# Six tiles in work in place of five, every engine's order and the PSUM banks written out per tile, early weights on ScalarE's DMA queue

## Time and profile before

| | |
|---|---|
| runs | 1672.52, 1680.17, 1679.59 us (median 1679.59) |
| profiled execution, first to last instruction (span) | 1672.2 us; the page gives no time beside it |
| TensorE busy | 1389.7 us, 83% |
| VectorE busy | 1370.5 us, 82% |
| ScalarE busy | 970.5 us, 58% |
| GpSimd busy | 721.2 us, 43% |
| mean granted TensorE clock | 0.956 |

### The profile page before, as it was taken

How to read it: one execution, slowest core, us unless ns; L and a number is a source line. 1 busy time by engine, 2 the same in 40 slices (tenths; PEclk the granted TensorE clock), 3 DMA queues, 4 the chain that set the end, 5 groups by cost and what they waited for, 6 DMA issues and landing times.

```text
span 1672.2 us, 42249 instructions
## 1 busy us (share of the span) xinstructions
PE 1389.7 (83%) x16237; PEld 973.1 (58%) x16270; DVE 1370.5 (82%) x4054; ACT 970.5 (58%) x1992; POOL 721.2 (43%) x1143
## 2 busy tenths in 40 slices
PE   2466789988888889999888889999888888997765
PEld 1344666666666666666565666666665666665432
DVE  4356798888988898888998898888988899887652
ACT  1134566666666666666566666666666666665432
POOL 4244454444544544444544544444544545442200
PEclk9888999999999999999999999999999999999875
DMA  6001111111111111111111110111111111111100
GB/s 211 10 8 28 39 25 34 43 43 43 30 43 42 42 28 29 43 43 43 30 43 43 43 32 25 43 43 43 33 39 43 42 37 23 29 33 31 28 24 4
DMA packets 130948, 64.36 MB, mean 38 GB/s; under 512 B 97591, under 2 KB 123575, under 8 KB 130494
## 3 DMA queue, kind: packets, MB, share of 16 engines
q1 hardware_dynamic: 130750, 61.66, 14.0%
HBM read 50.05 MB, written 2.14 MB: 31 GB/s over the span
## 4 chain that ended last, share of the span: by engine, by line
PE 46%; DVE 23%; POOL 11%; ACT 7%; issue 6%; SPq 4%; DMA 2%; POOLq 1%; DVEq 0%
PE ps_all L1332 7%; PE ps_all L1624 5%; PE ps_all L1458 5%; POOL rden L507 5%; POOL wide_a L507 4%; DVE mx L1013 4%; PE ps_all L1373 4%; PE ps_all L1444 4%; PE ps_all L1399 3%; DVE wide_b L1016 3%; PE ps_all L1325 3%; PE ps_all L1412 3%; DVE wide_b L1076 3%; POOL rstd L507 2%; DVE den L1061 2%
## 5 line engine op out<-in xcount | busy, mean ns | idle before, releaser
L507 POOL TENSOR_TENSOR rstd<-rstd,minus_half 128x1 f32<-128x1 f32 x320 | 175.6, 552 | 817.1 <-DVE rstd L991 814.1
L1013 DVE TENSOR_REDUCE mx<-ps_all 128x8 f32<-128x512 f32 (+1 forms) x192 | 163.8, 866 | 55.1 <-PE ps_all L1361 36.2
L507 POOL TENSOR_TENSOR rden<-rden,minus_half 128x16 f32<-128x16 f32 x64 | 187.7, 2933 | 9.4
L743 ACT COPY wide_a<-ps_all 128x512 f32<-128x512 f32 (+1 forms) x192 | 139.2, 725 | 88.4 <-PE ps_all L1412 72.7
L1332 PE MATMUL ps_all<-ident,wide_b 128*128 128x128 f32 x1024 | 156.4, 290 | 25.7 <-ACT wide_b L756 24.1
L507 POOL TENSOR_TENSOR wide_a<-wide_a,wide_b 128x256 f32<-128x256 f32 x256 | 177.7, 726 | 0.0
L1332 PEld LDWEIGHTS ps_all<-ident,wide_b 128*128 128x128 f32 x1024 | 121.4, 148 | 67.4 <-issue 34.2
L743 ACT COPY wide_c<-ps_all 128x512 f32<-128x512 f32 (+1 forms) x96 | 69.9, 728 | 118.3 <-PE ps_all L1332 118.3
L756 ACT ACTIVATE wide_b<-wide_b 128x512 f32<-128x512 f32 (+1 forms) x160 | 114.9, 718 | 23.8 <-DVE wide_b L1016 22.6
L1016 DVE TENSOR_TENSOR wide_b<-ps_all,mx 128x512 f32<-128x512 f32 (+1 forms) x160 | 126.0, 787 | 2.4
L1399 PE MATMUL ps_all<-w_qkv,ht_shift 128*128 128x512 f32 x256 | 124.1, 608 | 1.5 <-ACT ht_shift L766 1.5
(11 more groups left out here) (266 smaller groups left out, 3646.2 us busy)
## 6 DMA issues: line engine op xcount, KB each, us to landing
wide_a<-in_k SPq DMA_DIRECT2D x64, 256.0 KB, 3.1
wide_c<-wide_c SPq DMA_DIRECT2D x128, 64.0 KB, 2.2
v_pad<-in_v SPq DMA_DIRECT2D x32, 256.0 KB, 3.8
v_pair<-in_v SPq DMA_DIRECT2D x32, 136.0 KB, 2.7
ctx_t<-in_ctx_t SPq DMA_DIRECT2D x32, 128.0 KB, 2.3
ctx_s<-in_ctx SPq DMA_DIRECT2D x32, 128.0 KB, 3.1
xin<-in_x SPq DMA_DIRECT2D x32, 64.0 KB, 2.3
mask_row<-in_mask_f SPq DMA_DIRECT2D x32, 64.0 KB, 2.9
```

The costliest lines, as they stand in the source:

```text
L507: return gp.tensor_tensor(o, a, b, op)
L743: a.copy(to, of).then_inc(*done(name))
L1013: v.tensor_reduce(most, of, AX.X, ALU.max).then_inc(*done(f"{n}_max"))
```

## The change

- `G` goes from 5 to 6. The inputs of a tile and what is made of them for layer 1 (`xin`, `ctx_s`, `ctx_t`, `mask_row`, `plug`, `patches`, `pick`, `far`, `ctx_sq`, `ctx_rms`) get a count of their own, `EARLY = 4`; `first` of tile i loads the inputs of tile `i + 4`, and `picks` waits for `l1a_out` of tile `i - 4`.
- To make room, `kt`, `h_in` and `ot16` lie in `wide_c`; the setup's tensors lie in buffers of later tiles; the ternary weights take 3 planes for 4; GpSimd's DMA scratch is given as 1024.
- `PERIOD`, the times and the one table of banks go. `ORDER` has a symbol for each turn of each engine, which names the tile whose next stage is run; `BANK_TABLE` has a bank for each of the 32 tiles.
- The tensors of `soon` and `later` are issued by ScalarE, after `gate` and ahead of its wait for `pads`.
- A table load is issued ahead of the stage's wait, not behind it. The set with exp is now `exp_and_others`; the stages `l1f_tanh` and `l3f_bent` no longer ask for the GELU set. With the new order 107 loads are issued during the stages, where there were 70.
- The bias of layer 2's attention is put into rows 7 to 9 of `rows` once (one more DMA, and two selects, a memset and an addition on GpSimd in the setup), and the mask's matmul takes it along. Two matmuls per tile (line 1350) go.
- `l0a_k` of the two tiles `LATE` (now 4 and 5), not `l0a_sc`, waits for the prepared weights.

```diff
-G = 5
+G = 6
+EARLY = 4
-EXP_SET = "natural_log_exp_and_others"
+EXP_SET = "exp_and_others"
-PERIOD = 464
-PE_TIMES = """
-    l0a_kv 847, l0a_yt 901, l0a_q 920, l0a_sc 975, l0a_pt 1016, l0a_pv 1045, l0a_ot 1056, l0a_out 1073,
...
+ORDER = {
+    "pe": """
+        0000112031000100023121321132231013201303020012031220101301000132231232012012231013102301203203220321
...
-l0a_kv 0 1 l0a_k
+l0a_kv 02014643101177045502520415510437 1 l0a_k
...
+def in_turn(engine, lanes, once=None):
+
+    stages = {(lane, i): part(i) for lane, part in lanes.items() for i in range(TILES)}
+    if once:
+        stages["prep", 0] = once
+    for each in stages.values():
+        next(each, None)
+    for of in turns(engine):
+        next(stages[of], None)
...
-            load_weights(soon, "weights_soon")
-            load_first(2)
-            load_plug(2)
-            load_weights(later, "weights_later")
-            for i in range(3, G):
+            for i in range(2, EARLY):
                 load_first(i)
                 load_plug(i)
...
-                if i + G < TILES:
-                    yield "first"
+                yield "first"
+                if i + EARLY < TILES:
                     tile("l0a_x")
                     tile("picks")
                     tile("patch_sq")
-                    load_first(i + G)
-                    load_plug(i + G)
+                    load_first(i + EARLY)
+                    load_plug(i + EARLY)
...
+            for to, of in soon:
+                act.dma_start(to[:], of).then_inc(signal("weights_soon"), 16)
+            for to, of in later:
+                act.dma_start(to[:], of).then_inc(signal("weights_later"), 16)
             act.wait_ge(signal("pads"), 1)
...
                     yield f"{n}_exp"
+                    use(EXP_SET)
                     tile(f"{n}_sub")
-                    use(EXP_SET)
...
                 tile("l1f_mid")
-                use(GELU_SET)
...
                         mm(pair_of_banks(name, 256)[:, m], mask_sel[masks],
                            bc(rows[:, i * ROW:i * ROW + ROW], 1, 4), start=True, stop=False)
-                        if masks:
-                            mm(pair_of_banks(name, 256)[:, m], ones3, bc(bias_rows("logit", ROW), 1, 4),
-                               start=False, stop=False)
```

More of the change, by code:

```diff
@@ L53 @@
[L53 to L93, removed]
-    scaled3 1488, whole0 1514, whole1 1598, whole2 1659, whole3 1749, ternary0 1749,
-    ternary1 1816, ternary2 1898, ternary3 1936, tap0 1986, tap1 2003, tap2 2070
-    """
@@ L188 @@
+l3f_hid 73040017043260570757442641165003 1 l3f_act
+l3g_qt 65607262351252224744671434005146 1 l3g_qts
+l3g_out 57377362760716470145441724107003 1 l3f_x
+"""
 BANKS = {}
 for line in BANK_TABLE.strip().splitlines():
-    name, bank, n, *readers = line.split()
-    BANKS[name] = (int(bank), int(n), readers)
[L194 to L200, removed]
-        head = min(left, key=lambda h: (TIMES[h[0]][h[3]] + PERIOD * h[1], h[1]))
-        head[3] = next(head[2], None)
@@ L205, in all_tiles, with turns @@
-def all_tiles(lanes, *more):
-    in_turn(*((lane, i, part(i)) for lane, part in lanes.items() for i in range(TILES)), *more)
+    name, of_tile, n, *readers = line.split()
+    BANKS[name] = ([int(bank) for bank in of_tile], int(n), readers)
+def turns(engine):
+    main, side = LANES[engine]
+    for symbol in ORDER[engine].replace("\n", "").replace(" ", ""):
+        if symbol == ONCE:
+            yield "prep", 0
+        elif symbol in TILE:
+            yield main, TILE.index(symbol)
+        else:
+            yield side, SIDE.index(symbol)
@@ new lines, in positions @@
+def positions(engine):
+    stage, at = {}, {}
+    for turn, (lane, i) in enumerate(turns(engine)):
+        k = stage.get((lane, i), 0)
+        stage[lane, i] = k + 1
+        at[STAGES[lane][k], i] = turn
+    return at
+def in_turn(engine, lanes, once=None):
[6 more added lines that the diff above has]
+        next(stages[of], None)
@@ L341, in flamingo_stack @@
         k_part, quant_t = wide_a, wide_b[:, :, BANK:BANK + HID // 2].bitcast(BF16)
-        kt, h_in = ot16[:, :, 0, :], ot16[:, :, 1, :]
+        kt = h_in = wide_c[:, :, 0:P]
+        ot16 = wide_c[:, :, 0:2 * P].rearrange("p g (n e) -> p g n e", n=2)
         reach, decay = far[:, :, 0, :], far[:, :, 1, :]
@@ L431, in _ @@
             load_first(0)
-            load_weights(now, "weights_now")
+            for to, of in now:
+                sp.dma_start(to[:], of).then_inc(signal("weights_now"), 16)
             sp.dma_start(raw, d["tern"]).then_inc(signal("tern_in"), 16)
@@ L585, in _ @@
             tt(part8[:], part8[:], head16[:, 12:16], ALU.add)
+            with_bias = wide_b[:, 0, 0:P // 2].bitcast(BF16)
+            gp.memset(with_bias, 1.0)
+            gp.drain()
+            gp.affine_select(out=with_bias, in_=with_bias, compare_op=ALU.is_ge, fill=0.0, base=-7, pattern=[[0, P]],
+                             channel_multiplier=1)
+            gp.drain()
+            gp.affine_select(out=with_bias, in_=with_bias, compare_op=ALU.is_ge, fill=0.0, base=9, pattern=[[0, P]],
+                             channel_multiplier=-1)
+            gp.drain()
+            tt(row_sel[:, 1, :], row_sel[:, 1, :], with_bias, ALU.add)
             gp.memset(ht_shift[:], 0.0)
@@ L1627, in chain @@
                 yield from turn_many("l3g_round", "l3g_qt", wide_c[:, s, 0:HID], 4)
-                yield from down("l3g", 3)
-            all_tiles({"pe": chain})
+                yield from down("l3g", 2)
+            in_turn("pe", {"pe": chain})
 def rotary_table(np):
```

484 lines of the change are left out of this document (303 added, 181 removed).

## The result

The changed kernel's median is 1574.2 us (four runs, 1568.98 to 1582.68), beside 1676.05 (four runs, 1669.58 to 1680.17) for the kernel before on the same chip: a ratio of 0.9386, 95% interval 0.935 to 0.9422. It is faster by 6%. The forecast was 1555 us in 1512 to 1622, so the time lies 1.2% above it and inside the range. The profiled execution took 1568.98 us with a span of 1567.2; the forecast for that span was 1554.

What follows compares the result with a forecast made beforehand. TensorE and VectorE, equally busy, were taken to wait for each other. Head 242 + middle 1092 - 3 for matmuls + tail 221 + last store 2 = 1554 us span, plus 1: 1555 us, range 1512 to 1622.

Steps and rivals of the forecast that it cites:

- The bound: Middle: TensorE and VectorE, 89.2% and 89.4% busy, wait for each other; ends lose 74 and 57 us of TensorE.
- Order, head and tail: Ends: 54 and 58 more TensorE turns cost 15 us (bounds 0 to 36) and 18 us (0 to 38).
- Early weights: Head: weights issued on ScalarE's queue end tile 0's waits for `soon` and the half copy; net -12.5 us (0 to -15).
- Order, middle: Between tile 0's end and tile 31's start: engines 93.5% busy, 0.708 us per turn for 0.743, 1092 us (1063 to 1146).
- Two matmuls fewer: TensorE, each tile: 0.22 us less, 7 us in all, half counted: -3 us (bounds 0 and 17.5).
- More table loads: ScalarE: 107 loads for 70, 47 us more work, costed at nothing; 47 us at worst, gain of some 18 possible.
- Inputs with four sets: ScalarE's `patch_sq` waits for late inputs in most tiles, up to 5.6 us, borne by its 35% idle time.
- A: Rival, chance 0.2: fixed hand-overs keep the middle at 0.743 us per turn, only the ends gain; 1608 us.
- B: Rival, chance 0.13: middle 96% busy and half the charges at the ends; 1509 us.
- C: Rival, chance 0.08: late inputs hold ScalarE's queue and TensorE waits; slower than 1680 us, 1712 if all 5.6 us count.
- D: Rival, chance 0.07: real durations differ from the order's, six sets fill no better than five; 1640 to 1685 us.
- the likeliest case: Whole kernel: the forecast itself, 1555 us with its own range of 1530 to 1585, chance 0.52.

Runs made afterwards that it cites:

- the free order with five sets: The changed kernel with five sets of buffers and inputs, order and banks per tile found by exchanging neighbouring turns in a replay: 1643.42 us, 0.9781 of the kernel before.
- the change's second trace: The changed kernel run once more, nothing altered: 1577.1 us, 0.9408 of the kernel before; span of its trace 1579.4 us.
- the best order: The changed kernel with order and banks from a second round of exchanging turns: 1547.67 us, 0.923 of the kernel before.
- Two further orders: The changed kernel with only order and banks carried on by exchanging turns, in two rounds: 1552.13 us (0.9224), then 1547.67 us (0.923).
- the one-set kernel: The changed kernel with tanh in place of GELU in three places, so one table set and no table loads in the stages: 1567.0 us, 0.9321 of the kernel before.

## Why the prediction was right, and where it wasn't

**The bound.** Right. Both engines wait for each other, the ends are thin, and the order is what sets both: the old order under the new kernel is 0.3% faster than before, the new one 6%.

**Order, head and tail.** The turn counts were right, and the tail came within 3 us (223.8 for 221). The head's charge was wrong in sign. 54 more turns were to put 15 us in tile 0's way; but from its feed-forward's first transpose to its end (51.9 to 238.8 before, 45.2 to 221.2 after) tile 0 took 186.9 us before and 176.0 after, 26 us less than forecast. The same leg in other traces, as stretches with the columns of the earlier trace rows: the old order with the small edits, the free order with five sets, the change, and the change with its loads behind the wait.

```profile
49.95:238.41 188.46, 137.89 (x1393) 98.43 (x1395) 125.36 (x349) 83.18 (x174) 79.15 (x118) 0.87 0.09 21
45.23:217.67 172.44, 135.63 (x1381) 93.35 (x1385) 125.92 (x336) 82.40 (x176) 78.07 (x113) 0.87 0.11 27
45.20:221.24 176.04, 149.88 (x1782) 105.38 (x1782) 146.55 (x419) 108.09 (x220) 103.51 (x156) 0.97 0.14 34
47.25:235.63 188.38, 152.55 (x1778) 108.51 (x1782) 146.43 (x419) 108.22 (x220) 102.52 (x156) 0.95 0.13 32
```

From the first row to the second only the order and the banks differ, at the same clock and nearly the same number of turns (181 for 175 to tile 0's end): freedom of order takes 16 us off tile 0's own chain. That term is missing from the sum, which let the order act on tile 0 by crowding alone. From the second to the third come the sixth set and the crowding, 48 more turns: 3.6 us, or 6.6 with the change's second trace (179.1), at a clock of 0.97 and 0.96 for 0.87, and little more than traces of one order differ by. And it holds only with the table loads ahead of the wait: behind it the leg is 8 to 12 us longer than in four traces of this order with the loads ahead (176.0 to 180.8, among them those with the weights moved or held), while in the old order moving them ahead gained nothing here (188.5 for 186.9). The five-set row is one trace.

The tail is right partly by luck. The free order with five sets has a tail of 188.1 us, 15 under the one before; 60 more turns, with the sixth set, then add 36, near the upper bound of 38. The sum had no term for the first and half of the second.

No term of the sum has TensorE's clock either. In the head it was 0.90 and became 0.97, in the tail 0.82 and 0.89, so TensorE's work grew there by 18.7 us (144.5 to 163.1) and 32.4 (146.4 to 178.8), where the turns had been counted as 36 and 38.

**Early weights.** VectorE's wait for `soon` went, as did the late `v_pair`, but 6.7 of the 12.5 us came (51.9 to 45.2). The step that failed is the price of the move, of which the forecast says only that "what this queue move costs ScalarE is hidden in its wait for `pads`": I priced the move on the two engines and their queues, and not on the transfers that were under way on the other queue at that time. The weights delay `rows`, which were there by 20.06 us and now come at 25.65; so the first maximum stands at 33.20, not near 26, and the matmuls with `v_pair` at 38.34, not near 32. The 18 issues also took until 24.8, not 19.9: the first row of the fence has one of 2.41 us where the forecast took 0.48. The move alone is worth 6.6 us at this place (51.8 with the weights back on SyncE), or 5.5 by the change's second trace.

**Order, middle.** The term that decided the forecast was too good. 93.5% was taken and 91.4% came, 0.7265 us per turn for 0.708: 28 of the 31 us missing are this (0.0185 x 1542); the other 3 are the term for the two matmuls, which the measured rate already holds. The direction and the reason stand: the waits that came back in each tile are gone, and the longer gaps with them. The step allowed idle time of 6.5% of 1092 us, 71 us. The gaps under 0.5 us alone are 43.5 in the change and in the best order; the longer ones would have had to fall to 27, and came to 53 and 38. Two further orders reached 92.6% at best. Up to half of the rate's gain (13 of 25 us, by the estimate above) goes with the clock, of which the forecast says nothing.

**Two matmuls fewer.** Not resolvable by these runs, as its size would have it.

**More table loads.** Right within what can be measured, and for the reason given: all 107 cost nothing to 15 us against a kernel without any, and the 37 new ones a part of that; none of them begins after an idle wait. The gain of some 18 us, if half of the old 70 were in the way, didn't come: 35 were, and all small edits together brought 10 us at most. And the prediction priced only the count. That the same loads behind the wait would cost 77 us in this order stands nowhere in it, and its upper bound of 47 us, "cover gone", was short of it: there all loads behind an idle wait count, the old ones too (76 x 1.283 = 97.5). The Trainium skill, ScalarE: Activation LUTs, section "Table sets: the hidden batching unit", has a rule that speaks against this order, to batch activations by set. Here batching could win back at most the 15 us of the one-set kernel. The row of a load after the change shows again 1.28 us and nothing around it:

```profile
699.91 0.27 ACT L852 COPY ht<-ps_all 128x128 f32<-128x128 f32 x1 [0.28 <-PE ps_all L1435]
700.19 1.28 ACT L814 ACT_TABLE_LOAD   x1
701.49 0.63 ACT L865 ACTIVATE wide_b<-wide_b 128x512 f32<-128x512 f32 x1
```

The Trainium skill, ScalarE: Activation LUTs, section "What ACT_TABLE_LOAD costs", has 2.66 us per switch; an estimate from that figure is 285 us of ScalarE for 107 loads. The trace doesn't agree: the one-set kernel's ScalarE is 136 us less busy, which is 107 x 1.283 = 137.

**Inputs with four sets.** Right that it is harmless, wrong in how it looks. ScalarE was to stand in most tiles up to 5.6 us. All its waits for the context, beside the earlier trace rows: us in total, times, longest.

```profile
ACT far L829 <- DMA ctx_s<-in_ctx: 2.1, 3, 1.1
```

There are three, less than before. So the step that failed is the placing of ScalarE's turns against SyncE's on one scale of busy time; by how much it was off, no row shows.

**The rivals.** A, only the ends gain (1608): refuted by the rate, 0.7265 for 0.743, though nearer than I thought; the middle's gain is 54 us of rate in the forecast and 25 in the trace, of which 13 may be the clock's. With five sets the one trace is just A. B, fuller (1509): refuted, no order came near 96%. C, ScalarE held by late inputs (1712): refuted by the row above. D, it doesn't do what it says: refuted, though with the loads behind the wait (1651) the kernel comes to where D was put.

So the sum, 1554 for 1567.2, is good to 13 us by luck in part: a head 21 too dear stands against a middle 31 too cheap. The second trace (1579.4) would have it 25 us off, still inside the likeliest case's own 1530 to 1585.

## What to carry to other kernels

Where two engines are equally busy and waits are short and return in each tile at the same place, one more tile in flight with an order of its own for each tile can pay: here the two together brought 97 us, of which freedom of order without the extra tile had some 30, all at the ends. Put whatever needs no input (a table load) ahead of the wait, and the more so the more densely the order is packed: the same edit was worth at most some 10 us in the loose order and 77 in the packed one. Read the granted clock of each stretch before a change of rate is put down to the order. When bulk loads go to another queue, ask which small DMAs on the critical path are in flight then.

## What the runs showed of the hardware

- Bulk weights on one queue slowed a small DMA on another: the way of `rows` back from DRAM took at most 20.06 - 15.78 = 4.3 us alone, 6.8 beside the weights (18.89 to 25.65) and 8.4 with the weights issued at the same time (15.88 to 24.23); in the second case even its issue came 3.1 us later.
- The same weight's DMA (`w_in`) took 2.41 us to issue on ScalarE's queue and 0.60 on SyncE's; three others took 1.26 to 1.39 for 0.43.
- TensorE's granted clock has two levels in these records, full and half. The same line's 128x128 f32 matmul took 273 ns at full and 421 at half speed in the median, a 32x512 one 599 and 1067. Spans of one program go with it: the old order under the new kernel took 1665.2 us at 0.958 and 1682.0 at 0.947.
- One execution of the five-set kernel took 5203.59 us where the others took 1640 to 1653, with TensorE alone slower. Its trace has no records of the clock (its mean of 1.00 stands for none), so it can't say whether the clock was low. The rows are those of one matmul's line in it and in the change: count, shortest, median and longest ns.

```profile
L1490 PE MATMUL ps_all<-tern,wide_b x256: 222/527/750, 434.3 to 5199.1; 128*128 128x128 bf16 x128
```

```profile
L1490 PE MATMUL ps_all<-tern,wide_b x256: 216/219/314, 178.8 to 1564.6; 128*128 128x128 bf16 x128
```

VectorE was busy 1402 us there, near the 1359 to 1374 of the other traces, TensorE 5088.5. It came once; why is open.
